# Attention of a Trainium2 kernel with four heads' rows on the tensor engine at once, slopes on V, and V's products split by key tile over two steps

## The reference

```python
B, S, D, H, HD = 8, 256, 128, 16, 8
Q, K, V = x @ W_Q.T, x @ W_K.T, x @ W_V.T   # split in 16 heads
scores = Q @ K.T / sqrt(HD) + slope[h] * (key - query)    # key <= query, else masked
x = layernorm(x + (softmax(scores) @ V) @ W_O.T)
```

## Time and profile before

| | |
|---|---|
| time, median of 3 runs | 1690.85 us (1688.23 to 1693.26) |
| time of the profiled execution | 1694.99 us |
| its span | 1693.2 us |
| granted TensorE clock, mean | 0.852 of full |
| PE, DVE, ACT, POOL busy | 76%, 56%, 35%, 16% |

### The profile page before, as it was taken

One profiled execution on the slowest core, in us unless ns is written; L12 is line 12 of the kernel. 1 busy time (PEld: TensorE's weight loads), 2 busy tenths in 40 slices (PEclk: granted clock), 3 DMA queues, 4 the chain that ended last, 5 costly groups with the idle time before them and its releaser, 6 DMA issues. The chain is left out here.

```text
span 1693.2 us, 34235 instructions
## 1 busy us (share of the span) xinstructions
PE 1281.7 (76%) x11002; PEld 965.0 (57%) x11002; DVE 951.2 (56%) x3327; ACT 592.8 (35%) x1531; POOL 263.8 (16%) x280
## 2 busy tenths in 40 slices
PE   6999998999988113533699777699817897979782
PEld 4999996566645113510466452355405897979772
DVE  3666665344423776656645668444586265656423
ACT  3555552222220201132122121133311375757562
POOL 3322210000000000000000000222020343434332
PEclk9999998999999565666799878699957598989896
DMA  6996000000000000000172001333180121212111
GB/s 246 367 357 242 0 0 1 29 19 19 10 1 1 1 1 2 2 0 0 43 152 51 6 1 41 89 103 100 34 278 1 53 58 37 59 35 58 43 42 55
DMA packets 93077, 111.58 MB, mean 66 GB/s; under 512 B 13888, under 2 KB 66071, under 8 KB 92304
## 3 DMA queue, kind: packets, MB, share of 16 engines
q1 hardware_dynamic: 85200, 100.87, 19.7%
q0 software_dynamic: 7760, 9.25, 1.8%
HBM read 61.14 MB, written 53.43 MB: 68 GB/s over the span
## 5 line engine op out<-in xcount | busy, mean ns | idle before, releaser
L1654 PE MATMUL m_psY<-large,m_hT 128*128 x992 | 142.4, 288 | 4.8 <-issue 2.5
L1640 PE MATMUL m_psH<-m_xT,m_up 128*128 128x128 f32 x992 | 139.7, 286 | 0.0
L1654 PEld LDWEIGHTS m_psY<-large,m_hT 128*128 128x128 f32 x992 | 129.8, 195 | 5.6 <-issue 5.5
L1640 PEld LDWEIGHTS m_psH<-m_xT,m_up 128*128 128x128 f32 x992 | 129.3, 203 | 0.1
L1580 POOL DMA_INDIRECT rows<-m_ys,m_slot x93 | 90.4, 972 | 132.2 <-DVE m_slot L1848 117.3
L815 DVE SCALAR_TENSOR_TENSOR m_hid<-m_psU,m_wu,m_sg 128x512 f32<-128x512 f32 x64 | 48.1, 751 | 92.2 <-ACT m_sg L802 92.2
L1299 PE MATMUL m_acc<-se_place,se_parts 128*128 128x512 bf16 x384 | 89.5, 384 | 0.0
L1697 ACT ACTIVATE m_up<-large 128x512 f32 x124 | 78.1, 630 | 28.6 <-DVE m_valid L1751 17.2
L802 ACT ACTIVATE m_sg<-m_psG,m_wu 128x512 f32<-128x512 f32 x64 | 44.0, 687 | 123.3 <-PE m_psU L764 123.3
L424 ACT ACTIVATE at_Pr<-at_S,at_nmax 128x128 f32<-128x128 f32 x128 | 51.4, 402 | 98.8 <-DVE at_nmax L380 98.6
L776 PEld LDWEIGHTS m_psD<-m_wd,m_hid 128*128 128x128 f32 x512 | 67.0, 191 | 31.3 <-issue 30.4
(11 more groups left out here) (537 smaller groups left out, 2898.5 us busy)
## 6 DMA issues: line engine op xcount, KB each, us to landing
rows<-blank SPq DMA_DIRECT2D x2, 19584.0 KB, 103.2
m_xs<-rows SPq DMA_DIRECT2D x124, 76.5 KB
large<-in_L_attn_firs SPq DMA_DIRECT2D x4, 2048.0 KB, 16.6
large<-comb_rows SPq DMA_DIRECT2D x64, 128.0 KB, 5.2
se_wu<-in_L_ffn_up SPq DMA_DIRECT2D x32, 192.0 KB
W2T<-in_L_ffn_down_turned SPq DMA_DIRECT2D x1, 4096.0 KB, 12.5
large<-in_L_ffn_up SPq DMA_DIRECT2D x4, 1024.0 KB, 8.1
large<-in_L_ffn_down SPq DMA_DIRECT2D x16, 256.0 KB, 6.9
```

The lines of the kernel that those rows point to most:

```text
L1640: m = nc.tensor.matmul(psH[b][:, c * P:(c + 1) * P], up[b][:, c * P:(c + 1) * P], xT[b][:], start=True, stop=True)
L1654: m = nc.tensor.matmul(psY[b][:, 0:wide], hT[b][:, c * P:(c + 1) * P], k.W2[:, bass.ds(e + c * WIDE, wide)], start=(c == 0), stop=(c == C ...
```

## The change

- **Setup** also loads the four weights of attention, and fills two buffers with ones: `QA` on POOL and `KA` on DVE, each 128 by 8192. It makes the slopes times the key's place, and small tables of 16 columns.
- **Row groups.** `KA` and `QA` hold the 8 rows of each head at partition 0, 32, 64 or 96 of one of four groups. 16 transfers by SP and 16 by ACT put them there, out of `QT` and `KT`. Row 8 holds the slope times the key's place in `KA` and a one in `QA`; row 9 holds a one in `KA` and minus the row's maximum in `QA`. A product over 9 rows gives the scores with the slope, one over 10 rows the same minus the maximum, keys by queries, with nothing to transpose.
- **Two passes.** For head `u`, PE first writes the mask with two bf16 products (`hide_later`, L327 of the new file, one instruction for both diagonal tiles), then the scores (L334, L337); DVE takes the three maxima (L493). After 16 heads the maxima are turned by PE (L355, L357), copied by ACT (L448), and brought into row 9 by four transfers. For head `v`, 26 heads later, PE does `dots` (L344, L347), ACT the exponential straight out of PSUM (L455, with a bias column), and POOL zeroes the masked halves of the two diagonal tiles (L296). Two heads `u` and two heads `v` share a step of PE; their four row groups differ.
- **V.** `VA` holds V, multiplied by a table of the place inside the key tile and the head (the bias column takes it out of the exponential again), and a column of ones that gives the sums. `weigh(q, kt)` (L374) does one key tile of four heads, each to 32 columns of the array. Key tile 0 (256 queries) comes in one step and key tile 1 (128 queries) in the next; for every fourth quad both come in one step.
- **End of a sequence.** ACT copies the result (L464), PE turns it (L384), DVE divides (L479, L482).
- `KA`, `VA` and the weights live in the large buffer, so the load of `k.firs` moves to the end of the experts' stage and `clear_rows` to the block `ds` of the delta stage. W_O's rows are put in another order beforehand. The loop over sequences is written out for all 128 heads.

```diff
+            for w, n in ((k.at_wq, "Q"), (k.at_wk, "K"), (k.at_wv, "V"), (k.at_wo, "O")):
+                sp.dma_start(w, a[f"L0_attn_W_{n}"]).then_inc(k.tally("at_w_in").sem, 16)
...
+            nc.gpsimd.memset(k.at_QA[:], 1.0).then_inc(made.sem, 1)
+            nc.vector.memset(k.at_KA, 1.0)
...
+    TILES, GROUPS = 4, HEADS // 4
+    CAUSAL = 3 * P
+    LEAD = 26
+    PRING, TRING = 12, 3
+    ALL = BATCH * HEADS
+    QUADS = ALL // TILES
...
+            psS, psT, psO = ps[:, 0:4, :], ps[:, 4:7, :], ps[:, 7, :]
...
             @block.sync
             def _(sp):
+                for g in range(GROUPS):
+                    sp.dma_start(KA[HD:P:32, g, :].rearrange("i (b n) -> i b n", n=SEQ),
+                                 k.at_slopes[:, g, :].unsqueeze(1).to_broadcast([TILES, BATCH, SEQ])).then_inc(slopes_in.sem, 16)
+                sp.wait_ge(*q_out.at(4))
+                for g in range(GROUPS):
+                    for i in range(TILES):
+                        rows, head = slice(32 * i, 32 * i + HD), slice(32 * g + HD * i, 32 * g + HD * (i + 1))
+                        sp.dma_start(QA[rows, g, :], QT[head, :]).then_inc(rows_in[g].sem, 16)
                 start_delta_loads(k, a, sp)
+                for b in range(BATCH):
+                    sp.wait_ge(*peak_out.at(b + 1))
+                    for g in range(GROUPS):
+                        sp.dma_start(QA[9:P:32, g, b * SEQ:(b + 1) * SEQ], peakT[4 * g:4 * g + 4, b % 2, :])\
+                            .then_inc(peak_in[b % 2].sem, 16)
             @block.gpsimd
             def _(pool):
...
+                nc.gpsimd.memset(VA, 0.0).then_inc(cleared.sem, 1)
...
+                pool.wait_ge(*v_out.at(8))
+                nc.gpsimd.tensor_tensor(VA[:, :, :, 0:18], VA[:, :, :, 0:18],
+                                        k.at_weight[:].unsqueeze(1).unsqueeze(3).to_broadcast([P, T, HEADS, 18]),
+                                        ALU.mult).then_inc(cleared.sem, 1)
+                for v in range(ALL):
+                    pool.wait_ge(*expd.at(v + 1))
+
+                    nc.gpsimd.affine_select(out=diag(PT[:, v % PRING]), in_=diag(PT[:, v % PRING]), compare_op=ALU.is_ge,
+                                            fill=0.0, base=0, pattern=[[0, 2], [1, P]], channel_multiplier=-1)\
+                        .then_inc(cleared.sem, 1)
...
+                def hide_later(u):
+                    if u >= TILES:
+                        pe.wait_ge(*reduced.at(u - TILES + 1))
+                    out = psS[:, u % TILES, 0:CAUSAL].rearrange("p (x c) -> p x c", c=P)
+                    nc.tensor.matmul(diag(out), identb[:], maskb[:].unsqueeze(1).to_broadcast([P, 2, P]),
+                                     start=True, stop=False, skip_group_check=True)
+
+                def scores(u, part):
+                    b, g, r = operands(u)
+                    rows = slice(r, r + 9)
+                    if part == 0:
+                        return nc.tensor.matmul(psS[:, u % TILES, P:CAUSAL], QA[rows, g, keys(b, 1)],
+                                                KA[rows, g, b * SEQ:(b + 1) * SEQ],
+                                                start=False, stop=True, skip_group_check=True)
+                    return nc.tensor.matmul(psS[:, u % TILES, 0:P], QA[rows, g, keys(b, 0)], KA[rows, g, keys(b, 0)],
+                                            start=False, stop=True, skip_group_check=True).then_inc(scored.sem, 1)
+
+                def dots(v, part):
+                    b, g, r = operands(v)
+                    rows = slice(r, r + HD + 2)
+                    if part == 0:
+                        return nc.tensor.matmul(psT[:, v % TRING, 0:SEQ], KA[rows, g, keys(b, 0)],
+                                                QA[rows, g, b * SEQ:(b + 1) * SEQ], start=True, stop=True,
+                                                skip_group_check=True)
+                    return nc.tensor.matmul(psT[:, v % TRING, SEQ:CAUSAL], KA[rows, g, keys(b, 1)],
+                                            QA[rows, g, keys(b, 1)], start=True, stop=True,
+                                            skip_group_check=True).then_inc(dotted.sem, 1)
+
+                def turn_peaks(b):
+                    pe.wait_ge(*peaked.at(b + 1))
+                    if b == 0:
+                        pe.wait_ge(*v_out.at(8))
+                    nc.tensor.matmul(psO[0:HEADS, SEQ:SEQ + P], peaks[:, b % 2, :, 0], minus[:],
+                                     start=b == 0, stop=True, skip_group_check=True)
+                    nc.tensor.matmul(psO[0:HEADS, SEQ + P:2 * SEQ], peak1[:, b % 2, :], minus[:],
+                                     start=False, stop=True, skip_group_check=True).then_inc(turned.sem, 1)
+
+                def weigh(q, kt):
+                    b, quad = divmod(q, GROUPS)
+                    if kt == 0:
+                        pe.wait_ge(*cleared.at(4 + TILES * (q + 1)))
+                        if quad == 0:
+                            pe.wait_ge(*v_out.at(8))
+                            pe.wait_ge(*(normed.at(b) if b else peak_out.at(1)))
+                        if quad == 1 and b + 1 < BATCH:
+                            pe.wait_ge(*peak_out.at(b + 2))
+                    half = quad // 2 * SEQ
+                    for i in range(TILES):
+                        h, slot = TILES * quad + i, (TILES * q + i) % PRING
+                        o = psO[32 * i:32 * i + 32, half + kt * P:half + SEQ]
+                        x = PT[:, slot, 2 * kt:2 + kt, :].rearrange("p x c -> p (x c)")
+                        m = nc.tensor.matmul(o, VA[:, 2 * b + kt, h, :], x, start=quad % 2 == 0 and kt == 0,
+                                             stop=quad % 2 == 1 and kt == 1, skip_group_check=True)
+                    if kt == 1:
+                        m.then_inc(weighted.sem, 1)
+
+                def turn_raw(b):
...
+                    pe.wait_ge(*raw_out.at(b + 1))
+                    for qt in range(2):
+                        for half in range(2):
+                            o = qt * SEQ + half * P
+                            m = nc.tensor.transpose(psO[:, o:o + P], raw[:, b % 2, half * SEQ + qt * P:half * SEQ + (qt + 1) * P],
+                                                    k.ident[:])
+                    m.then_inc(raw_turned.sem, 1)
+                for step in range(-LEAD // 2, ALL // 2 + 4):
+                    us = [u for u in (2 * step + LEAD, 2 * step + LEAD + 1) if 0 <= u < ALL]
+                    vs = [v for v in (2 * step, 2 * step + 1) if 0 <= v < ALL]
+                    for u in us:
+                        if u < HEADS and u % TILES == 0:
+                            pe.wait_ge(*rows_in[u // TILES].at(128))
+                        hide_later(u)
+                    for v in vs:
+                        b, n = divmod(v, HEADS)
+                        if n == 0:
+                            pe.wait_ge(*peak_in[b % 2].at(64 * (b // 2 + 1)))
+                        if v == 0:
+                            pe.wait_ge(*v_out.at(8))
+                        if v >= TRING:
+                            pe.wait_ge(*expd.at(v - TRING + 1))
+                    for part in range(2):
+                        for u in us:
+                            scores(u, part)
+                        for v in vs:
+                            dots(v, part)
+                    done = 2 * step + 2
+                    if done == HEADS + TILES - LEAD:
+                        turn_peaks(0)
+                    q, late = done // TILES - 2, done % TILES == 2
+                    if 0 <= q < QUADS:
+                        if not late:
+                            weigh(q, 0)
+                        if late == (q % GROUPS != GROUPS - 1):
+                            weigh(q, 1)
+                            if q % GROUPS == 0 and q // GROUPS + 1 < BATCH:
+                                turn_peaks(q // GROUPS + 1)
+                    if done % HEADS == 6 and HEADS < done:
+                        turn_raw(done // HEADS - 1)
             @block.scalar
             def _(act):
+                nc.scalar.activation(k.at_weight[:], k.at_bias[:], ACT.Exp, scale=-1.0)
...
+                act.wait_ge(*k_out.at(4))
+                for g in range(GROUPS):
+                    for i in range(TILES):
+                        rows, head = slice(32 * i, 32 * i + HD), slice(32 * g + HD * i, 32 * g + HD * (i + 1))
+                        act.dma_start(KA[rows, g, :], KT[head, :]).then_inc(rows_in[g].sem, 16)
+                act.wait_ge(*cleared.at(3))
...
+                def copy_peaks(b):
+                    act.wait_ge(*turned.at(b + 1))
+                    if b >= 2:
+                        act.wait_ge(*peak_in[b % 2].at(64 * (b // 2)))
+                    nc.scalar.activation(peakT[:, b % 2, :], psO[0:HEADS, SEQ:2 * SEQ], ACT.Copy).then_inc(peak_out.sem, 1)
+
+                copy_peaks(0)
+                for v in range(ALL):
```

(88 more changed lines are left out.)

255 lines of the change are left out of this document (88 added, 167 removed).

## The result

| | before | after |
|---|---|---|
| time, median | 1690.71 us (4 runs) | 1719.47 us (4 runs, 1718.19 to 1719.91) |
| span of the profiled execution | 1693.2 us | 1717.8 us |
| granted TensorE clock, mean | 0.852 | 0.786 |

What follows compares the result with a forecast made beforehand. TensorE's order was taken as the bound. Attention's end: 26.5 + 16 + 113 + 9 + 5 + 5 = 174.5 against 256.7, -82, and +1 for the clearing: 1614 us profiled, 1610 median; range 1588 to 1660.

Steps and rivals of the forecast that it cites:

- drops of the clock: Attention: loss to falls of TensorE's granted clock, taken as 5 us in the sum.
- Side by side, and the loop at full clock: Attention loop: four row groups overlap fully, priced at full clock; 64 steps at 1.76 are 113 us.
- The rows' part: Scores and dots of four heads in a loop step: 0.65 us with full overlap, 2.6 with none.
- the extras of each sequence: Attention, per sequence: turning maxima, transposes and the wait behind norm, together 1.1 us, eight times 9 us.
- 3.07 times for four row tiles: Rule against the forecast, on the loop's row part: about 0.86, the kernel some 13 us slower, 1623.
- Against the clock: Argument against half clock in the loop: high through dense small products, yet slices 14 to 18 show 5 and 6 tenths.
- The rival that named the cause: Loop partly serial, by queued weight loads or half clock: steps 2.3 to 3.0, +35 to +75, 1645 to 1685; chance 0.17.
- the sign: Listed mark of a wrong forecast: a granted clock near 0.5 in slices 1 to 4.
- The start: Before the loop: first scores at 26.5 against 30.97, remaining groups 1.9 us apart, 13 scores-only steps at 1.22, 16 us.
- The clearing: clear_rows moved into ds: 0 to 15 us, 1 taken; its +15 rival, 1625, shared chance 0.27 with threefold overlap.
- The cover named: In ds, SP's wait of 66.5 us was to hide clear_rows' issue of 62.6 us, with 4 us left.
- the waits that I had named: PE's waits without releaser in ds, most likely for instructions; full transfer engines could lengthen them, 0 to 15 us, 1 taken.

Runs made afterwards that it cites:

- e1: The changed kernel with all 32 rows of a row group in scores and dots, not 9 and 10; 1650.4 us, 0.9769 of the kernel before.
- f1: The changed kernel with 32 rows in scores and dots and the clearing in eight pieces in the attention; 1612.7 us, 0.9620 of the kernel before.
- e4: The changed kernel plus 34 full products keeping PE busy before the four waits for row transfers; 1738.8 us, 1.0258 of the kernel before.
- f3: The changed kernel with 16 rows in scores and dots, not 9 and 10; 1707.0 us in one run, 1.018 of the kernel before.
- g2: f1 with heads v 24 instead of 26 behind heads u, so both use the same two row groups; 1761.3 us, 1.0496 of the kernel before.
- f4: f2 plus unread 32-row products in free row groups in the steps before the first dots; 1616.4 us, 0.9638 of the kernel before.
- f2: f1 with row transfers cut in two by tokens, first halves of all heads sent first; 1604.1 us, 0.9585 of the kernel before.
- e2: The changed kernel with the clearing in eight pieces behind the attention's peak transfers, not in ds; 1697.0 us, 1.0029 of the kernel before.

## Why the prediction was wrong

It said 174.5 for the end of the attention and +1 behind it; it was 262.5 and +19. The 88 us in the attention are 24 up to the first dots, 68 in the loop and 1 behind it, less the 5 taken for drops of the clock. By its own steps:

- **Side by side, and the loop at full clock: right.** The rows' part was to be 0.65 with 0.11 for the first load and 0.12 for the shape: 0.88. It is 0.87 in e1. The 64 steps with the extras of each sequence were to take 113 + 9 = 122; they took 186.7 - 69.3 = 117.4 in e1 and 119.7 in f1. The exponential takes 0.578 (forecast 0.58). So this part is confirmed only by the runs with 32 rows; in the changed kernel itself the clock hid it. The Trainium skill (TensorE: Matmul & The Clock Gate, Measured speedup vs the span model) has 3.07 times for four row tiles. As the prediction used it, with load and shape on top of it, it does not show: the row part would be 1.09. But with load and shape counted in, four heads in 0.87 against 0.65 for one are 4 x 0.65 / 0.87 = 3.0 times, and so the Trainium skill's number and this trace agree.
- **The clock: the step that failed.** The failed term is "Drops of the clock ... I take 5 us", and under the rival "Against the clock: it stays high through slices of dense small products". Those slices hold products over all 128 rows of the array, or, at `ds` and `dt`, have a clock of 5 and 6 tenths, which I put down to PE's gaps. The rival that named the cause ("because little of the array is used") had 2.3 to 3.0 us a step, and it was 189.9 / 64 = 2.97. But I gave it a part of 0.17 and let it end at 1685 (64 times 3.0 - 1.76 is 79, not 75, so 1689), since I did not put its half clock on the 13 first steps, nor add the two misses below. What the runs showed in place of the 5 us is half clock throughout the loop, 189.9 - 117.4 = 72.5 us of it by e1. The prediction named the sign ("a granted clock near 0.5 in slices 1 to 4"), but gave its price to the rival only.
- **The start: mis-sized.** The remaining groups were to arrive 1.9 us apart. They came 7.5, 6.8 and 5.0 apart, since I priced the transfers by their issues (0.47 each; they took 0.75 on SP's queue and 0.8 on ACT's) and not by what they move: 2 MB in 28 us, 75 GB/s, with the small loads of the delta stage beside them from 33 us on. (Those are 15, not the 17 of the prediction.) With the first at 30.8, not 26.5, and the 13 steps at 2.12 instead of 1.22, the first dots came at 66.3 instead of 42.5: 24 us, of which halves of the rows gave 11 back.
- **The clearing: mis-sized, and beyond its upper end.** 1 us taken, 0 to 15 given, 18.8 measured. The cover named (SyncE waits 66.5 us in `ds`) hid the issue, 48.9 us, but not the bytes. `ds` became 9.4 us longer, mostly by the waits that I had named and priced near nothing; the transfers then ran on into `dt` (0.45 of the engines there), where I had counted nothing, for another 9.4.
- **Right and free:** `k.firs` behind the experts; the experts and filters kept their lengths. The weights in setup brought the projection from 15.15 to 12.6.

That the clock follows the rows of the array in use is shown for this loop by e1, e4, f3, g2 and f4. What is open: in e1, f1 and f2 it stayed high through the last steps, which have dots in two groups only, beside V's products over all 128 rows; in f4's profiled execution it fell in the same steps. And one drop of 3.4 us in f4's loop (96.5 to 99.9 us) has no cause that the trace shows.

## What to carry to other kernels

A product's time is not the whole price of using few rows of the array: before a change goes from full tiles to row groups, ask what it does to the rows in use at a time, and pad the operands with rows that do no harm; here 32 rows took no longer than 9 at the same clock (2.12 us a first step with either). Read the granted clock beside the busy share; a PE that is busy throughout at 0.50 is the sign. A large transfer that is moved should be priced by where its last byte falls, not by its issue, and row transfers of a few partitions by their bytes.

## What the hardware showed that I had not expected

- Granted clock of stretches in which PE was busy nearly throughout: four groups of 9 and 10 rows 0.50, four of 16 rows 0.50, two of 32 rows 0.50 (g2; also the first steps of e1, where PE was busy for 28.6 of 35 us), four of 32 rows 1.00. Mask products over all 128 rows stood between them in each. The Trainium skill, TensorE: Matmul & The Clock Gate, Part 1, ties the gate to how busy PE has been; here PE was busy 110.00 of 110 us at 0.50, so busy as the profile counts it did not suffice.
- 39 MB of clearing made two blocks of small products 18.8 us longer, by later instruction packets; in the attention it cost nothing at half clock (e2) and 2.3 us at full clock (f1).
- Transfers of 8 rows of 8 KB inside SBUF, on two queues, moved 75 GB/s (106 GB/s with the small loads beside them, from 22 to 50 us), against 357 GB/s for the clearing in `ds`.
